# GpSimd ends each layer norm of a two-layer decoder, and a norm of a norm shares one set of sums

## The reference

```python
def _layernorm(x, axis=-1, eps=1e-05):
    m = jnp.mean(x, axis=axis, keepdims=True)
    v = jnp.var(x, axis=axis, keepdims=True)
    return (x - m) / jnp.sqrt(v + eps)
...
    def _L1_xattn_ref(xx, ee, ...):
        def _ln(x, g, b):
            m = jnp.mean(x, -1, keepdims=True)
            v = jnp.var(x, -1, keepdims=True)
            return (x - m) * jax.lax.rsqrt(v + 1e-05) * g + b
        def _mha(x, y, ...):
            xn = _ln(x, lnx_g, lnx_b)
            yn = _ln(y, lny_g, lny_b)
            ...
            x_out = x + o @ li1_w + li1_b
            h = jax.nn.gelu(_ln(x_out, ln3_g, ln3_b) @ li2_w + li2_b, approximate=False)
            return x_out + h @ li3_w + li3_b
        x = _ln(xx, ln1_g, ln1_b)
        x = x + _mha(x, x, ...)
        x = _ln(x, ln2_g, ln2_b)
        return x + _mha(x, ee, ...)
    x = _layernorm(x + _L0_attn_ref(x, ...))      # splat attention
    x = _layernorm(x + _L0_xattn_ref(x, ctx_512, ...))
    x = _layernorm(x + _L0_ffn_ref(x, ...))       # eight experts, best one
    x = _layernorm(x + _L1_attn_ref(x, ...))      # causal attention
    x = _layernorm(x + _L1_xattn_ref(x, ctx_512, ...))
    x = _layernorm(x + _L1_ffn_ref(x, ...))       # sixteen experts, best four
    return x
```

## Time and profile before

| | |
|---|---|
| time before, median of 3 runs | 3960.23 us (3958.79 to 3975.51) |
| profiled execution: its own time | 3954.29 us |
| its span | 3952.6 us |
| PE busy | 3343.7 us, 85% |
| DVE busy | 2807.9 us, 71% |
| ACT busy | 2094.5 us, 53% |
| POOL busy | 975.9 us, 25% |

### The profile page before, as it was taken

How to read it: one execution, slowest core, us unless ns; L and a number is a source line. 1 busy time by engine, 2 the same in 40 slices (tenths; PEclk the granted TensorE clock), 3 DMA queues, 4 the chain that set the end, 5 groups by cost and what they waited for, 6 DMA issues and landing times. The chain is left out here.

```text
span 3952.6 us, 94629 instructions
## 1 busy us (share of the span) xinstructions
PE 3343.7 (85%) x38960; PEld 2374.8 (60%) x38960; DVE 2807.9 (71%) x6362; ACT 2094.5 (53%) x4222; POOL 975.9 (25%) x1808
## 2 busy tenths in 40 slices
PE   1889888989898888888988888899888898988886
PEld 1666565666565656656656656566655665655554
DVE  5777776777776767777776667677776677777664
ACT  4745565455556554564564555645555556455551
POOL 0312341122222321131132222212342112124310
PEclk9989888988898889888988988898988898989887
DMA  5000000000000000000000000000000000000000
GB/s 163 3 3 2 2 3 4 9 7 3 2 2 2 8 3 7 7 3 2 7 2 2 5 4 7 6 4 2 1 2 3 9 9 4 2 2 2 1 4 6
DMA packets 30365, 31.49 MB, mean 8 GB/s; under 512 B 8673, under 2 KB 26482, under 8 KB 29938
## 3 DMA queue, kind: packets, MB, share of 16 engines
q1 hardware_dynamic: 29938, 25.44, 2.1%
HBM read 21.24 MB, written 4.19 MB: 6 GB/s over the span
## 5 line engine op out<-in xcount | busy, mean ns | idle before, releaser
L1103 ACT ACTIVATE p<-bank,p_log 128x512 f32<-128x512 f32 (+2 forms) x1280 | 746.8, 583 | 1331.3 <-PE bank L797 1266.6
L1669 POOL TENSOR_TENSOR prob<-p,prob 120x256 f16<-120x256 f32 (+2 forms) x512 | 455.5, 890 | 1742.4 <-ACT prob L1104 1741.3
L1104 ACT ACTIVATE prob<-bank,p_log 128x512 f16<-128x512 f32 (+2 forms) x1280 | 747.3, 584 | 0.0
L1368 DVE TENSOR_REDUCE negm<-bank 128x2 f16<-128x512 f32 (+1 forms) x1280 | 675.3, 569 | 33.9 <-PE bank L752 18.2
L1286 DVE TENSOR_TENSOR prob<-p,prob 128x512 f16<-128x512 f32 (+2 forms) x768 | 474.0, 624 | 188.9 <-ACT prob L1104 178.8
L774 PE MATMUL bank<-q,k 32*128 32x256 f16 (+2 forms) x6144 | 496.8, 289 | 65.1 <-issue 34.7
L668 PE MATMUL bank<-w_exp,ident_h 128*128 128x512 f16 x1280 | 429.3, 421 | 32.3 <-DVE negm L1368 15.2
L1678 POOL TENSOR_SCALAR_AFFINE_SELECT probm<-prob 128x128 f16<-128x128 f16 x1024 | 325.9, 358 | 340.4 <-DVE prob L1286 340.4
L774 PEld LDWEIGHTS bank<-q,k 32*128 32x128 f16 (+1 forms) x6144 | 307.9, 110 | 142.7 <-issue 66.8
L797 PE MATMUL bank<-ident_h,negm 128*128 128x256 f16 (+2 forms) x2560 | 384.9, 273 | 0.0
L1661 POOL TENSOR_TENSOR rstd<-veps,minus_half 128x2 f32<-128x2 f32 (+1 forms) x208 | 149.7, 720 | 887.9 <-DVE veps L1261 887.3
(11 more groups left out here) (300 smaller groups left out, 6286.5 us busy)
## 6 DMA issues: line engine op xcount, KB each, us to landing
x<-in_x SPq DMA_DIRECT2D x16, 256.0 KB, 2.7
out<-z SPq DMA_DIRECT2D x16, 256.0 KB, 2.2
xa<-in_li SPq DMA_DIRECT2D x9, 256.0 KB, 4.6
x<-in_li SPq DMA_DIRECT2D x7, 256.0 KB, 4.3
z<-in_wq SPq DMA_DIRECT2D x4, 256.0 KB, 4.4
z<-in_li SPq DMA_DIRECT2D x4, 256.0 KB, 4.1
cx<-in_ctx_t SPq DMA_DIRECT2D x16, 60.0 KB, 1.8
cx<-in_ctx SPq DMA_DIRECT2D x16, 60.0 KB, 1.8
```

Of the source, the lines that this page charges most:

```text
L1103: act(p32[0:n, g % PBUF32, 0:cols], ps[0:n, 0:cols], ACT.Exp, bias=p_log[0:n, :], scale=a.scale)
L1104: act(prob[0:n, 0, g % PBUF, 0:cols], ps[0:n, 0:cols], ACT.Exp, bias=p_log[0:n, :], scale=a.scale).then_inc(a_done, one(a_done))
L1368: v.tensor_reduce(negm[:, h * NT:(h + 1) * NT], ring_v[bank_of(e, v_full)][:, :].rearrange("p (t n) -> p t n", t=NT)[:, :, 0:ATTNS[k].keys ...
L1669: g.tensor_tensor(prob[0:n, 1, m % PBUF, 0:cols], p32[0:n, m % PBUF32, 0:cols], prob[0:n, 0, m % PBUF, 0:cols], ALU.subtract).then_inc(pp_ ...
```

## The change

The two `tensor_scalar` operations that end a norm go from DVE to POOL, right behind the root. For k = 3 the first norm and the norm of its result use one set of sums: with variance v of x, the variance of the normed x is v/(v + eps), so that both at once are x minus mean times the root of 1/(v(1 + eps) + eps^2). POOL then takes a power of four columns and makes four `tensor_scalar` operations. The pieces for DVE alone go from the tables, the piece `norm2` too, `norm3` of k = 3 moves from turn 17 to turn 16, and `norm_end` of `norm4` (turn 20) is now part of `norm3`. DVE waits for a norm's result in `gain` and, two norms back, before it reuses `mv`. The wait for the output DMA of a `z` buffer moves from DVE to POOL.

```diff
-    3: (("oT", 9), ("out", 12), ("norm2", 15), ("norm3", 17), ("norm4", 20)),
+    3: (("oT", 9), ("out", 12), ("norm3", 16)),
...
-VECTOR_ONLY = ("out2", "experts3", "norm4", "h3", "r3", "ctx2")
...
+                def norm_begin(src, ready, n=P, nt=NT, twice=False):
+
+                    i = len(norms) % 2
+                    if len(norms) >= 2:
+                        e.wait_ge(*norms[-2])
...
+                    if twice:
+                        v.tensor_scalar(veps[i][0:n, nt:2 * nt], mv[i][0:n, 0:nt, 1], 1.0 + EPS, EPS * EPS,
+                                        ALU.mult, ALU.add).then_inc(dve_step, one(dve_step))
...
-                def norm_end(number, src, dst, ready=dve_step, n=P, nt=NT):
-
-                    i = (number - 1) % 2
-                    e.wait_ge(rstd_ready, number)
-                    for t in range(nt):
-                        signal = dve_step if t < nt - 1 else ready
-                        v.tensor_scalar(dst[0:n, t, :], src[0:n, t, :], mv[i][0:n, t, 0:1], rstd[i][0:n, t:t + 1],
-                                        ALU.subtract, ALU.mult).then_inc(signal, one(signal))
-                    e.wait_ge(dve_step, sent(dve_step))
-                    e.wait_ge(ready, sent(ready))
...
                 def gain(s):
 
+                    e.wait_ge(*norms[-1])
...
                         elif k == 3:
                             add_bank(x[s], x[s])
-                            number = norm_begin(x[s])
+                            norm_begin(x[s], xn_ready, twice=True)
...
                         if k == 3:
-                            norm_end(number, x[s], x[s])
-                            number = norm_begin(x[s])
-                            yield
-                            norm_end(number, x[s], xa[s])
                             gain(s)
-                            number = norm_begin(xa[s])
-                            yield
-                            wait_sent(k, b)
-                            norm_end(number, xa[s], zk, z_ready[s])
+                            norm_begin(xa[s], z_ready[s])
                             yield
...
-                def root(n=P, nt=NT):
+                def norm(src, dst, ready, n=P, nt=NT, again=None):
 
                     e.wait_ge(var_ready, upcoming(e, var_ready))
                     i = sent(rstd_ready) % 2
-                    g.tensor_tensor(rstd[i][0:n, 0:nt], veps[i][0:n, 0:nt],
-                                    minus_half[0:n, 0:nt], ALU.pow).then_inc(rstd_ready, one(rstd_ready))
+                    cols = nt if again is None else 2 * nt
+                    g.tensor_tensor(rstd[i][0:n, 0:cols], veps[i][0:n, 0:cols],
+                                    minus_half[0:n, 0:cols], ALU.pow).then_inc(rstd_ready, one(rstd_ready))
+                    e.wait_ge(rstd_ready, sent(rstd_ready))
+                    for to, c in ((dst, 0),) if again is None else ((again, nt), (dst, 0)):
+                        for t in range(nt):
+                            last = g.tensor_scalar(to[0:n, t, :], src[0:n, t, :], mv[i][0:n, t, 0:1],
+                                                   rstd[i][0:n, c + t:c + t + 1], ALU.subtract, ALU.mult)
+                    last.then_inc(ready, 1)
```

104 lines of the change are left out of this document (45 added, 59 removed).

## The result

| | before | after |
|---|---|---|
| median | 3961.95 us (4 runs, 3958.79 to 3975.51) | 4182.63 us (4 runs, 4175.77 to 4188.16) |
| PE's idle time in the profiled execution | 609 us | 776 us |
| PE busy | 3343.7 us | 3407.8 us |

The ratio is 1.0549 with a 95% interval of 1.0519 to 1.058: the kernel became 5.5% slower. The prediction was 1.8% faster, and the time lies outside its range. All times are of the chip's faster state; one run of the second kernel of experiment 2 fell in the slower one (5050.65 us at a granted clock of 0.551) and is left out, and as that kernel's trace is of this run, only GpSimd's times are read from it.

The account below looks back on a forecast made before the run. PE was the backbone, bound by idle time in which DVE, late in places, ended over half its waits. Terms -35 - 30 - 10 + 12 + 3 - 10 = -70 us gave 3890 us, 1.8% less; range 3835 to 3962.

Parts of the forecast that it names:

- (a): Chain of k = 3: PE's waits for row maxima behind DVE's norms shrink 2.2 us, 16 times; -35 us, ends 0 and -51.
- (b): The other 160 norms: DVE freed of 172 us, so PE waits less for its other work; -30 us, ends 0 and -87.
- (c): Norm results for PE: one POOL tensor_scalar of 128x256 takes p = 0.50 us, results come slightly earlier; -10 us over 62 waits.
- Both ends: Bounds for the norm-result waits: -29 us at p = 0.40 (select), +8 us at p = 0.70 (two inputs).
- (d): POOL's queue: each norm holds up low parts or masks 2p = 1.0 us more; +12 us, ends 0 and +69.
- (e): Interference: DVE operations lengthened beside POOL, some tens of us, grow by a fifth; +3 us on PE.
- (f): PE's clock: with less idle time the 21% share at 1.2 GHz falls a little; -10 us, other end 0.
- slow GpSimd: Rival: POOL's operation costs well above its neighbours; break-even at p = 1.02 us, near 4000 us at p = 1.2; chance 0.10.
- The lock: Rival: SBUF lock with DVE holds each of POOL's two operations 0.25 us; -24 us, about 3936 us; chance 0.20.
- The hidden case: Rival: PE, relieved of DVE, meets ACT's exponentials or its own order; no change, about 3956 us; chance 0.12.
- The signs: Profile values expected after the change, among them 400 POOL operations near 500 ns and PE's idle time near 540 us.
- three marks of being wrong: p near 1 us; waits for low parts and masks more than double; ACT takes over waits that DVE gave up.

Follow-up runs that it names:

- experiment 2: Changed kernel with POOL ending norms, mean left in, by one tensor_tensor multiplication: 3919.36 us; second kernel, by a tensor_scalar of one operation: 4057.55 us.
- experiment 4: Kernel before, DVE still ending norms, with idle POOL filler behind each root: long (four operations, 2.9 us) 4122.26 us; short (two, 1.2 us) 3960.26 us.
- experiment 1: Kernel before with 33 extra POOL operations after its last norm, each waited for; tensor_scalar of 256 columns with two per-partition operands took 1.26 us.

## Why the prediction was wrong

**What bounds the kernel** was read rightly: DVE is late in places, not full. When it was relieved of 178 us, PE's other waits for it fell by 48.8 us, 14.7 of them at `negm` of the row scores. What was not seen is that POOL stands so near the path of PE that the waits only change their engine: with the operation at the price of the prediction (experiment 2) PE waits 35.5 us less for DVE's other work and idles as long as before.

**Terms (a) and (b)**, -65 us together, were of the right kind: the two waits of the k = 3 chain are gone in the timeline, and -48.8 us stand in the ledger. Their size is not shown by that. With the long filler of experiment 4, where DVE keeps the norms, these waits also fell, from 227.5 to 199.2 us, perhaps because a PE that waits for POOL arrives later at DVE's results.

**Term (c) is the step that failed.** It took p = 0.50 us from a select and bounded it by a `tensor_tensor` at 0.70; measured was 1.25, and 1.26 with nothing beside it (experiment 1). That price decides the sign: with the operation at 0.53 us the same kernel gains 38 us, at 1.27 it loses 221 (experiment 2). "Both ends" were two other kinds of instruction, neither a `tensor_scalar`. The only row that spoke of arithmetic with many steps, the root with 0.72 us for two columns, was quoted against it and then given 0.10. With p put right, the form of (c) holds fairly well: 62 x (2.50 - 1.27) = +76 us against the +99 of the ledger, with 77 waits instead of 62.

**Term (d) was mis-sized**, and its form was wrong. By 24p it would be +30 us at the true price; the ledger has +144.5. Three things were left out. The cost rises faster than the hold: 1.2 us cost nothing on balance, 2.9 us 160 us (experiment 4). ACT also waits for POOL's low part, since `p` may not be overwritten before (from 4.1 to 122.6 us), and that holds up the exponentials that follow. And for k = 3 only the last norm was reckoned, as 4 us within a pair's 6.2; the root and four operations ahead of it hold the queue for 6.4 us (377.15 to 383.59), which uses up the cover, and the wait of 4.01 us stands there.

**Term (e)** was too small on DVE. With the shared sums alone DVE is busy 2792.3 us; less the 211.8 us of its norm ends that is 2580.5, and it came to 2629.7. So what DVE kept takes 49 us longer, where a fifth of some tens of us had been reckoned. POOL's busy time is not the measure for it: with the multiplication of experiment 2 POOL is busy 268 us less (1193.3 us), but DVE 33 us more (2662.4), most of it at the line of the low parts, L1276 (593 against 554 us). That kernel is the fastest of all, so this weighs little there; what it costs PE in the changed kernel no run shows. On POOL the operations are hardly longer beside DVE (1.27 us) than alone (1.26).

**Term (f) had the wrong sign.** The granted clock fell from 0.895 to 0.865, so PE was at 1.2 GHz for 27% of the time instead of 21%, and it was busy 64 us longer instead of 10 shorter. In the runs with an idle time of 604 to 635 us the clock is between 0.887 and 0.907 and PE's busy time between 3297 and 3364 us; in those with 706 to 778 us, the changed kernel among them, it is 0.857 to 0.876 and 3393 to 3426 us. More idle time goes with a lower clock, but it is not all: the multiplication by the root idles as long as the kernel before and is 47 us less busy. A forecast for idle time alone therefore leaves out a good part of what is lost here: 64 of 231.5 us in the changed kernel, 69 of 170 with the long filler.

**The rivals.** The first, slow GpSimd, is what happened, with a chance of 0.10 and a time "near 4000" at p = 1.2. Even at the right p its terms give 3962 - 72 + 76 + 30 = 3996, a growth of 34 us; the span grew by 231.5. Of the 197 us between, (d) has some 115, (f) 74, (c) 23, (a) and (b) 16, less the 32 us by which PE's waits for nothing shown fell. Its break-even of p = 1.02 was really at 0.65 (experiment 2). The lock is not what made POOL slow, since its price is its own. The hidden case holds in part: at the price of the prediction PE's idle time did not fall, but the waits passed from DVE to POOL and not to ACT, as that rival had it (experiment 2).

**The signs.** `negm` (48.5 us) and the count of 400 came out as forecast, the others not: 1250 ns and not 500, POOL at 1461 and not 1165 us, `probm` at 104.5 and not 50 to 60, norm results at 206 and not 95, DVE's busy time at 2630 and not 2585, PE's idle time at 776 and not 540. Two of the three marks of being wrong appeared: p above 1 us, and waits for low parts and masks 3.5 times as long. ACT did not take over (94.7 to 98.1 us).

**What stays open.** How the loss of the changed kernel divides exactly between late results and held queue: the ledger says +99 and +144.5 on PE, but the measured prices of either alone (205 us for results 1.5 us later, 160 us for a hold of 2.9 us) come from kernels in which DVE ends the norm, overlap, and can't be added. Why the three forms of experiment 2 lie near one line although the two fillers do not is open too; the fillers' effect on DVE's norm ends may be a part of it. Whether a version whose tiles have zero mean by construction, so that one multiplication of 1.07 us ends a norm, can be made without losing the 38 us elsewhere was not tried. Nor do these runs show why the clock of that kernel is higher at the same idle time.

## What to carry over

Before work is moved to an engine, find or measure the very instruction there, with its kind of operands; a neighbour of the same size can be off by a factor of 2.5, and an experiment of a few microseconds would have settled it. In an in-order program count what the moved work delays twice, as a result that comes late and as a hold of the queue behind it, and ask of each how much cover there is: here results 1.5 us later cost 205 us, a hold of 1.2 us nothing on balance, one of 2.9 us 160 us. An engine with much idle time that stands between two others at every step has less room than its share says. And look what else a filler changes before its run is taken for the price of one thing.

## What the runs showed of the hardware

- POOL, 128 partitions f32 with 256 columns: copy 0.40 us, `tensor_tensor` 0.72, `tensor_scalar` 0.92 with one per-partition operand and one operation, 1.07 with two constants, 1.26 with two per-partition operands; writing f16 instead of f32 changed little (1.22).
- The power took 0.66 us for one column of 120 partitions, 0.72 us for two of 128 and 1.16 us for four, so one instruction for two norms saved only 0.28 us.
- `tensor_tensor` with the root broadcast along 512 columns took 1.04 to 1.09 us on POOL, less than half of the two `tensor_scalar` operations that it stood for; beside it DVE's low parts were longer (593 against 554 us in all at L1276).
- DVE's 400 norm ends took 206.8 us in the kernel before, 158.7 to 160.0 us where a filler kept POOL's low parts away from them, and 238.8 us where the filler stood ahead of the root: the same instructions, 0.40 to 0.60 us each by what POOL does beside them.
